# A rotation stage reordered: means through a selecting matrix in TensorE column groups, high and low halves stacked for one projection

## The reference, cut to what matters

```python
h_mean = jnp.mean(x, axis=1)                     # x here is layernorm(x): (32, 128, 256)
params = h_mean @ omega_proj_w.T + omega_proj_b  # fills an antisymmetric 64 x 64 omega per sample
G = I + omega + 0.5 * omega2 + 1.0 / 6.0 * omega3
x_rotated = jnp.einsum('bld,bde->ble', x[:, :, :64], G)
lie_out = x_rotated @ omega_out_w.T + omega_out_b
vq_input = h_mean @ vq_proj_in_w.T + vq_proj_in_b
...                                              # nearest code, projected: vq_contribution
out = residual + omega_mix * lie_out + vq_mix * vq_contribution
return out * jax.lax.rsqrt(jnp.mean(out * out, -1, keepdims=True) + 1e-6) * norm_w
```

## Time and profile before

| | us |
|---|---|
| median of three runs | 1541.12 |
| lowest and highest of them | 1536.94, 1543.99 |
| the profiled execution | 1539.01 |
| its span, first to last instruction | 1536.6 |
| mean granted clock of TensorE in it | 0.876 |

### The profile page before, as it was taken

One profiled execution on the slowest core, in us unless ns is written; L12 is line 12 of the kernel. 1 busy time (PEld: TensorE's weight loads), 2 busy tenths in 40 slices (PEclk: granted clock), 3 DMA queues, 4 the chain that ended last, 5 costly groups with the idle time before them and its releaser, 6 DMA issues. The chain is left out here.

```text
span 1536.6 us, 30143 instructions
## 1 busy us (share of the span) xinstructions
PE 1248.9 (81%) x10831; PEld 917.1 (60%) x10831; DVE 1007.9 (66%) x2050; ACT 728.4 (47%) x1401; POOL 416.5 (27%) x403
## 2 busy tenths in 40 slices
PE   4989589898744379999999828894699976999997
PEld 2666357766633369999999727842455542565664
DVE  5998658776644846666666475556788786567553
ACT  4777445564334124444444323033255556756742
POOL 2222255545221034545545301043011111000000
PEclk9999799999975579999999955555899997999999
DMA  7766277655418022323322180000643321133131
GB/s 274 245 237 232 99 142 121 124 103 85 57 70 372 0 76 91 94 91 100 113 76 82 44 322 30 2 1 24 157 94 83 64 37 57 64 130 109 45 125 28
DMA packets 100041, 165.03 MB, mean 107 GB/s; under 512 B 14902, under 2 KB 63802, under 8 KB 98620
## 3 DMA queue, kind: packets, MB, share of 16 engines
q1 hardware_dynamic: 90876, 138.20, 32.3%
q0 software_dynamic: 8640, 24.65, 5.0%
q10 hardware_dynamic: 384, 0.26, 0.1%
HBM read 110.61 MB, written 52.30 MB: 106 GB/s over the span
## 5 line engine op out<-in xcount | busy, mean ns | idle before, releaser
L1545 DVE TENSOR_TENSOR r_sim<-r_pS,r_causal 128x512 f32<-128x512 f32 x128 | 86.4, 683 | 56.0 <-PE r_pS L1455 55.8
L1087 POOL DMA_INDIRECT expert_results<-mt_yout,m_deliver x78 | 77.4, 993 | 151.8 <-ACT mt_yout L1175 139.8
L1120 PE MATMUL mt_pU<-mt_xh,m_w 128*128 128x256 f16 x624 | 116.2, 274 | 1.5 <-DVE mt_xl L1205 1.5
L1120 PE MATMUL mt_pV<-mt_xh,m_w 128*128 128x256 f16 x624 | 116.2, 274 | 0.0
L2955 ACT ACTIVATE q_ex<-q_pE 128x512 f32<-128x512 f32 x128 | 75.7, 600 | 83.3 <-PE q_pE L2574 83.2
L2670 DVE TENSOR_REDUCE q_mx<-q_pS 128x4 f32<-128x512 f32 x128 | 87.3, 686 | 32.0 <-PE q_pS L2553 31.6
L1131 PE MATMUL mt_pY<-m_w,mt_hh 128*128 x624 | 106.4, 273 | 1.0 <-DVE mt_hl L1219 1.0
L3237 PE MATMUL s_pY<-s_w,s_hh 128*128 128x256 f16 x576 | 99.9, 273 | 8.0 <-DVE s_hl L3457 6.6
L1169 ACT ACTIVATE mt_hh<-ahead 128x512 f16<-128x512 f32 x78 | 49.2, 630 | 119.4 <-DVE ahead L1214 119.4
L1079 POOL DMA_INDIRECT mt_xin<-token_rows,m_fetch x78 | 86.2, 1104 | 68.2 <-POOLq L778 44.7
L1211 DVE TENSOR_TENSOR ahead<-mt_pU,ahead 128x512 f32<-128x512 f32 x78 | 54.0, 692 | 58.3 <-ACT ahead L1163 58.3
(11 more groups left out here) (587 smaller groups left out, 3504.4 us busy)
## 6 DMA issues: line engine op xcount, KB each, us to landing
s_spread_share<-shares SPq DMA_DIRECT2D x32, 512.0 KB, 5.4
a_pf<-in_L_ffn_W SPq DMA_DIRECT2D x24, 512.0 KB, 6.1
m_w<-split_w SPq DMA_DIRECT2D x6, 2048.0 KB, 22.9
split_w<-a_ph SPq DMA_DIRECT2D x24, 256.0 KB, 3.8
split_w<-a_pl SPq DMA_DIRECT2D x24, 256.0 KB, 4.2
r_kstack<-k_bounce SPq DMA_DIRECT2D x48, 128.0 KB, 4.1
r_qstack<-q_bounce SPq DMA_DIRECT2D x48, 128.0 KB, 5.4
q_Q<-m_bounce SPq DMA_DIRECT2D x24, 256.0 KB, 7.5
```

The source lines that it names most:

```text
L1087: pool.indirect_dma_start(results[:, :], bass.IndirectOffsetOnAxis(ap=deliver[:, at:at + 1], axis=0), yout[n % 2][:, a, :], None).then_inc ...
L1120: last = pe.matmul(ps[half][:, j, :], W[x][:, e, dc, cols], (xh, xl)[y][p][:, dc, :], start=(m == 0), stop=(m == len(steps) - 1))
L1545: dve.tensor_tensor(sim[n % SIMS][:, :].rearrange("p (h t) -> p h t", t=S), pS[n % 2][:, :].rearrange("p (h t) -> p h t", t=S), repeat(tab ...
```

## The change

The diff has four parts. (1) `stats(h)` comes ahead of `low(2h-2)` in DVE's loop. (2) The means: DVE fills a matrix `pick` with zeros and puts 1/128 into eight places, so that block g of 32 columns selects row g. For each of the four places q in a group one float32 matmul with this block as stationary operand and the 256 features of the sample as moving operand adds into partitions 32q to 32q+31 of PSUM, over all groups. After the last group ACT copies the 128 x 256 sums out, TensorE transposes them in two steps, and ACT reads the means from there. (3) The projection: the weights Woo lie twice, on partitions 0 to 63 and 64 to 127, by one more DMA of 64 KB; the low half of the rotated rows is written to partitions 64 to 127 under the high half, so that one matmul with 128 rows takes the place of two with 64. (4) The four samples of a group are done in two pairs, each in the order shift, shift, stacked, stacked, low, low.

```diff
-        mix, ones, half = c.sb("mix", [P, 2]), c.sb("ones", [P, 1]), c.sb("half", [P, 1])
+        mix, half = c.sb("mix", [P, 2]), c.sb("half", [P, 1])
+        pick, mean_rows = Wp[:, 0:NG * ONES], Wp[:, NG * ONES:NG * ONES + D]
...
+        pSum = banks[0][:, 0:D]
+        pM = banks[3][:, 0:DC * P].rearrange("p (a n) -> p a n", a=DC)
+        by_sample = pM.rearrange("p a (q r) -> p a r q", q=GB)[:, :, 0:NG, :]
...
+                for half_at in (0, LD):
+                    sp.dma_start(Woo[half_at:half_at + LD, :], A["L1_attn_Woo"]).then_inc(s["w_in"], 16)
...
-                    for b in range(g * GB, g * GB + GB):
-                        for dc in range(DC):
-                            last = pe.matmul(pM[:, dc, b:b + 1], XN[:, b, dc * P:(dc + 1) * P], ones[:, :],
-                                             start=True, stop=True)
+                    for q in range(GB):
+                        last = pe.matmul(pSum[q * ONES:(q + 1) * ONES, :], pick[:, g * ONES:(g + 1) * ONES],
+                                         XN[:, g * GB + q, :], start=(g == 0), stop=(g == NG - 1))
...
-                    for b in range(GB):
-                        pe.matmul(pY[g % 2][:, b, :], ones16[:, :], shift_rows[:, g * GB + b, :], start=True, stop=False)
-                        for n, (x, w) in enumerate(TERMS):
-                            last = pe.matmul(pY[g % 2][:, b, :], xr[g % 2][x][:, b * S:(b + 1) * S], Woo16[w][:, :],
-                                             start=False, stop=(n == 2))
+                    for pair in ((0, 2), (1, 3)):
+                        for b in pair:
+                            pe.matmul(pY[g % 2][:, b, :], ones16[:, :], shift_rows[:, g * GB + b, :], start=True, stop=False)
+                        for b in pair:
+                            tokens = slice(b * S, (b + 1) * S)
+                            pe.matmul(pY[g % 2][:, b, :], xr[g % 2][:, tokens], Woo16[0][:, :], start=False, stop=False)
+                        for b in pair:
+                            tokens = slice(b * S, (b + 1) * S)
+                            last = pe.matmul(pY[g % 2][:, b, :], xr[g % 2][0:LD, tokens], Woo16[1][:, :], start=False,
+                                             stop=True)
...
                 last.then_inc(s["meant"], 1)
-                pe.wait_ge(s["w_in"], 16 * 10)
+                pe.wait_ge(s["mean_rows"], 1)
+                for dc in range(DC):
+                    last = pe.transpose(pM[:, dc, :], mean_rows[:, dc * P:(dc + 1) * P], ident[:, :])
+                last.then_inc(s["mean_turned"], 1)
+                pe.wait_ge(s["w_in"], 16 * 11)
...
                 act.wait_ge(s["meant"], 1)
-                act.activation(hm[:, :, :], pM, ACT.Copy).then_inc(s["kept"], 1)
+                act.activation(mean_rows[:, :], pSum, ACT.Copy).then_inc(s["mean_rows"], 1)
+                act.wait_ge(s["mean_turned"], 1)
+                act.activation(hm[:, :, :].rearrange("p a (r q) -> p a r q", q=GB), by_sample, ACT.Copy)\
+                   .then_inc(s["kept"], 1)
...
-                    dve.scalar_tensor_tensor(xr[g % 2][1][:, :], pR[g % 2], 1.0 / GSCALE, xr[g % 2][0][:, :],
+                    dve.scalar_tensor_tensor(xr[g % 2][LD:P, :], pR[g % 2], 1.0 / GSCALE, xr[g % 2][0:LD, :],
                                              ALU.mult, ALU.subtract).then_inc(s["xr_low"], 1)
...
-                dve.memset(ones[:, :], 1.0 / S).then_inc(s["ones"], 1)
+                step(dve.memset(pick[:, :], 0.0))
+                dve.memset(pick[:, 0:(NG - 1) * (ONES + 1) + 1:ONES + 1], 1.0 / S).then_inc(s["ones"], 1)
...
                     add(2 * h + 1)
+                    stats(h)
                     low(2 * h - 2)
-                    stats(h)
                     low(2 * h - 1)
```

More of the change, by code:

```diff
@@ L1843, in lie_rotation @@
         bp, sign = c.sb("bp", [LD, LD]), c.sb("sign", [LD, LD])
-        Wvi, Wvo, Woo = c.sb("Wvi", [P, DC, LD]), c.sb("Wvo", [LD, D]), c.sb("Woo", [LD, D])
-        Woo_mixed = c.sb("Woo_mixed", [LD, D])
-        Woo16 = [c.sb(f"Woo16{t}", [LD, D], f16) for t in range(2)]
+        Wvi, Wvo, Woo = c.sb("Wvi", [P, DC, LD]), c.sb("Wvo", [LD, D]), c.sb("Woo", [P, D])
+        Woo_mixed = c.sb("Woo_mixed", [P, D])
+        Woo16 = [c.sb("Woo16h", [P, D], f16), c.sb("Woo16l", [LD, D], f16)]
         bvi, bvo, boo = c.sb("bvi", [B, LD]), c.sb("bvo", [B, D]), c.sb("boo", [B, D])
@@ L1863, in lie_rotation @@
         ones16 = ones_rows[LD:LD + 2, :]
-        xr = [[upper[0:LD, 2 * D + (2 * i + t) * GT // 2:2 * D + (2 * i + t + 1) * GT // 2].bitcast(f16) for t in range(2)]
-              for i in range(2)]
+        xr = [upper[:, 2 * D + i * GT // 2:2 * D + (i + 1) * GT // 2].bitcast(f16) for i in range(2)]
         ss, me, rr = (c.sb(n, [P, 2, GB]) for n in ("ss", "me", "rr"))
@@ L1888, in lie_rotation @@
         s = {n: c.sem(n) for n in (
-            "consts_in w_in wp_in ones added1 added2 stat summed scaled ve rstd shifted xn turned high low meant kept "
+            "consts_in w_in wp_in ones added1 added2 stat summed scaled ve rstd shifted xn turned high low meant mean_rows mean_turned kept "
             "hm_high hm_low half_made norms step vq_projected vnorm cnorm both_turned turned_kept "
@@ L1908, in _ @@
                 sp.dma_start(nw, A["L1_attn_norm_w"].partition_broadcast(P)).then_inc(s["consts_in"], 16)
-                for t, n in ((Wvi, "L1_attn_Wvi"), (code, "L1_attn_codebook"), (Wvo, "L1_attn_Wvo"), (Woo, "L1_attn_Woo"),
-                             (behind, "behind"), (bp, "L1_attn_omega_b"), (sign, "sign")):
+                for t, n in ((Wvi, "L1_attn_Wvi"), (code, "L1_attn_codebook"), (Wvo, "L1_attn_Wvo"), (behind, "behind"), (bp, "L1_attn_omega_b"), (sign, "sign")):
                     sp.dma_start(t[:], A[n]).then_inc(s["w_in"], 16)
+                for half_at in (0, LD):
+                    sp.dma_start(Woo[half_at:half_at + LD, :], A["L1_attn_Woo"]).then_inc(s["w_in"], 16)
                 for t, n in ((bvi, "L1_attn_vq_proj_in_b"), (bvo, "L1_attn_vq_proj_out_b"), (boo, "L1_attn_omega_out_b")):
@@ L2042, in xr_high @@
                         act.wait_ge(s["rotated"], g - 1)
-                    act.activation(xr[g % 2][0][:, :], pR[g % 2], ACT.Copy, scale=1.0 / GSCALE).then_inc(s["xr_high"], 1)
+                    act.activation(xr[g % 2][0:LD, :], pR[g % 2], ACT.Copy, scale=1.0 / GSCALE).then_inc(s["xr_high"], 1)
                 def squares(g):
@@ L2235, in _ @@
                 dve.wait_ge(s["consts_in"], 48)
-                dve.wait_ge(s["w_in"], 16 * 10)
+                dve.wait_ge(s["w_in"], 16 * 11)
                 step(dve.tensor_scalar(nw16, nw, float(D) ** 0.5, None, ALU.mult))
-                mark(dve.tensor_scalar(Woo_mixed[:, :], Woo[:, :], mix[0:LD, 0:1], WSCALE, ALU.mult, ALU.mult), "woo_mixed")
+                mark(dve.tensor_scalar(Woo_mixed[:, :], Woo[:, :], mix[:, 0:1], WSCALE, ALU.mult, ALU.mult), "woo_mixed")
                 low(NG - 2)
@@ L2288, in _ @@
                 dve.wait_ge(s["woo_high"], 1)
[L2289 removed]
+                dve.tensor_tensor(Woo16[1][:, :], Woo_mixed[0:LD, :], Woo16[0][0:LD, :], ALU.subtract).then_inc(s["woo_low"], 1)
                 keep_square(0)
```

5 lines of the change are left out of this document (2 added, 3 removed).

## The result

| | before | after |
|---|---|---|
| median, us (4 runs each) | 1539.03 | 1525.02 |
| lowest and highest | 1535.87, 1543.99 | 1523.98, 1526.54 |
| profiled execution, us | 1539.01 | 1524.42 |
| its span, us | 1536.6 | 1522.0 |
| mean granted clock in it | 0.876 | 0.884 |

What follows compares the result with a forecast made beforehand. DVE's loop and TensorE's means were taken to bound the front part, TensorE the rotation part, with POOL's add close behind. -7.5 to the means and -3.1 in the rotation gave -10.6 us: 1530 us, range 1524 to 1537.

Steps and rivals of the forecast that it cites:

- Statistics ahead of low: DVE's loop in the front part: the 1.23 us idle time disappears in each iteration, -4.3 us.
- Means: Front part, TensorE: column groups side by side take 1.0 us per group, not 3.27; -4.4 us, +1.15 for copy and transposes.
- the forecast's 6.15 and 1.15: Last pair: sums ready 6.15 us after ACT's first row; copy, two transposes and handovers add 1.15.
- Middle part: Between means and rotation part: no instruction changes but the scaling of Woo, so it moves as a whole.
- Projection: Rotation part, TensorE: 12 matmuls per group for 16, 4.64 us for 5.71; 3.1 us gained, 5.5 of 8.6 lost.
- the ring: Rotation part: ACT's squares and root, then POOL's add before z is rewritten; limits each group to 5.51 us.
- (a): Rival, rotation part: POOL's limit doesn't hold and TensorE stays the limit; -16.1 us, 1525; chance 0.09.
- (b): Rival, means in the front part: column groups run serially, 4.27 us of TensorE per group; 1536; chance 0.10.
- (c): Rival, means in the front part: each column group drains, 0.63 us per instruction; net +0.5, 1541.6; chance 0.03.
- (d): Rival, layer behind the stage: 40 us of full clock run at half; net +7.6, 1549; chance 0.04.

Runs made afterwards that it cites:

- e1: Changed kernel with DVE's loop order as before, the statistics behind the first low again: stage 155.84 us, 4.04 longer; median 1530.61, ratio 0.995.
- e4: Changed kernel with the selecting matmuls of the means all in one column group instead of four: stage 149.95 us, 1.85 shorter; median 1520.42, ratio 0.991.
- e9: Changed kernel with an own buffer for ACT's squares, plus unread filler products behind each group's means: stage 148.06 us, median 1520.49, ratio 0.988.
- e12: Changed kernel with an own buffer for ACT's squares, plus unread filler products only where TensorE waits anyway: stage 139.55 us, median 1511.40, ratio 0.985.
- e5: Changed kernel with ACT's squares written to an own buffer, so they don't wait for POOL's add: stage 146.27 us, median 1519.30, ratio 0.989.
- e11: Changed kernel with the own buffer for squares but the projection as before (16 matmuls per group): stage 153.91 us in one execution, 7.6 longer than e5.
- e10: Changed kernel with the own buffer for squares, stacked projection done sample by sample instead of in pairs: 5.31 us per group, stage 150.81, one execution.

## Why the prediction was right

The forecast was 1530 us with a range from 1524 to 1537; measured are 1525.0, close to the lower end. In the stage, where the forecast was worked out, it had -10.6 us, and -11.65 came.

**Statistics ahead of low.** Right: -4.18 for -4.3, the idle time gone (e1 brings it back). It holds only with the short means: with the old ones the shift is 0.98 later.

**Means.** Right: 1.0 us per group for 1.0. From ACT's first row to the means 7.14 us pass (934.37 to 941.51), and the forecast's 6.15 and 1.15 are 7.3. The bound of 3.41 for no overlap was near e4's 3.55. The Trainium skill ("TensorE: Matmul & The Clock Gate", section Part 3: Packing small matmuls) says that weight loads overlap running matmuls only where the row group differs. The trace doesn't agree. In the changed kernel all eight use all rows, and their weight loads are done at 937.68, while the first four products run from 937.48 to 938.12:

```profile
937.48 0.20 PEld L1934 LDWEIGHTS l_pair<-l_XN,l_Wp 128*32 128x32 f32 x8 [0.38 <-issue]
```

**Middle part.** This is the term that was mis-sized. It was put at no change of its own, "moves as a whole", and was 1.09 us shorter, of which 1.00 lies in the 144 products that ran in part at the high clock. The forecast took the 0.50 of the whole stretch for a property of the stage ("all of the stage before is on the low level now and stays there") and looked for the clock only behind it. It depends on what TensorE did in the stretch before, as e9 and e12 show. That the missing term helped and did not cost was luck.

**Projection.** Right in mechanism and size: 4.64 us per group, squares from group 2 on 5.5 apart and waiting for POOL, -3.0 for -3.1. e5 and e11 show both sides of it: TensorE's saving was 7.6 us, 4.7 of which the ring took. The forecast had 8.6 and 5.5, since it gave every group the full 1.07; without the ring squares of group 0 came 0.89 earlier and the last distance was 0.31 shorter. Both numbers were mis-sized by about the same, which is why their difference came out right. The 0.108 us per change of rows, worked out from one sample of project, was confirmed by e10. DVE's low part, written to the upper 64 partitions, takes the 0.68 us that was assumed. Finish takes 2.79 beside the add, for 2.69 from the earlier trace rows. The Trainium skill ("SBUF — State Buffer", section Who interferes with whom) says that a DVE instruction with two inputs in SBUF contends with a GpSimd instruction that reads SBUF. The trace agrees: finish has two such inputs and takes 2.79 us in place of 1.66, while take, which has one in PSUM, keeps its 1.23 beside the same add (1006.06). No run varies the inputs alone.

**The rivals.** (a) did not come: the ring held, at 5.51 as worked out. (b) did not come, and was mispriced. Serial column groups were put at -4.8 us; e4 shows -13.5, since at the high level the eight take 1.9 us and the omega part is 3.3 shorter than in the changed kernel. The rival was worked out at the low level alone. (c) is excluded by the rows of the last pair, where the eight take 1.0 us and not 5. (d) did not come: behind the stage the two spans agree to 0.1 us.

**The total.** 1525.0 lies 5.5 us under the unrounded 1530.5. Of these, 2.1 are the median of before, which came out at 1539.0 and not 1541.1. Of the other 3.4 (14.0 measured for 10.6) the stage accounts for 1.05, and the rest is scatter. By the later rounds before stands at about 1536.3; from there the forecast's 10.6 lead to 1525.7. So the difference was forecast well, and most of the 5.5 us lies in the few executions of before from which the sum was taken.

## What to carry to other kernels

Follow the chain to the second limit before you book a saving: here a ring of two engines stood 0.2 us behind TensorE and took over half of its gain, and one buffer of its own, worth nothing before, gave it back. TensorE's low clock in a stretch of short, scattered products is no constant: a stretch can be priced at either level, and products in the waits ahead of a long run of small matmuls can be worth more than the work that was saved (6.7 us here, for 5.4 by the new means), if they delay nothing. Put them where the engine waits anyway, and check in the profile that no other engine gets a new wait.

## What the runs showed of the hardware

- Eight float32 instructions of 256 moving columns, to four column groups with all 128 rows in use, took 1.01 us to the next start at the low clock and 0.57 at the high one (e12, 940.22 to 940.79); to one column group 3.55 and 1.85 (e4).
- The omega products, 128 rows by 64 stationary and 32 moving columns, also follow the clock: 144 took 7.86 us at the low clock (55 ns each) and 4.71 at the high one (33 ns).
- A change of the number of rows between matmuls costs 0.11 us at the low clock, whether the rows grow or shrink (e10: 2 to 128, 128 to 64, 64 to 2).
- A faster way to compute the same can lengthen the stage. With four column groups TensorE stood idle for 4.87 us ahead of group 6 and had the high clock for 3.4 us around the first omega products; with one (e4) it stood idle for 1.73 us, had the high clock from 932.5 to 949.7 us, and the stage was 1.85 us shorter.
